# Two feed-forward up-projections of a four-block attention kernel: from a plain fp32 product to three rounded products over 128 rows

## The chip, the cores and the metric

One core of a Trainium2 chip. The metric is the device time of one execution in microseconds (us); the time before is the median of three runs. Engines: TensorE (PE in the rows; PEld is its weight load), VectorE (DVE), ScalarE (ACT), GpSimd (POOL) and SyncE (SP), on whose queue all DMAs of this kernel are issued.

## The reference

Four attention blocks run one after another on four batches of 256 rows of 160 values, with a context of 512 rows of 96 values (`B, SQ, D = 4, 256, 160`, `SK, C = 512, 96`). Blocks L1 and L3 are transformer blocks and end in a gated feed-forward half:

```
h1 = _ln(x, n1_g, n1_b)
x = _attn(h1, h1, q1, k1, v1, o1_w, o1_b, heads) + x
h2 = _ln(x, n2_g, n2_b)
x = _attn(h2, context, q2, k2, v2, o2_w, o2_b, heads) + x
h3 = _ln(x, n3_g, n3_b)
proj = h3 @ ff_w1 + ff_b1
a, g = jnp.split(proj, 2, axis=-1)
ff = a * jax.nn.gelu(g, approximate=False) @ ff_w2 + ff_b2
return ff + x
```

`ff_w1` is 160x1280 and `ff_w2` 640x160. Blocks L0 and L2 are attention with a residual; L2 adds a small second attention over four extra rows. All is fp32.

## The kernel before, in words

The work is 24 instances: six phases (`PHASES`) by four batches. Phase 0 is L0's attention, 1 and 2 the self and cross attention of L1, 3 the block L2 (with the small attention, unit 4), 4 and 5 those of L3. In an instance the heads go by fours (a "quad"). For a quad the keys are brought into a ring of four slots by four DMAs (`kdma`, ring L901); TensorE makes the scores once for the row maximum (`max`, L972, reduced on VectorE at L1428), transposes the negated maximum into the queries (`mtr`, L986, added at L1452), makes the scores again transposed (`st`, L952), ScalarE takes the exponential (`probs`, L1259), and TensorE multiplies by the values (`pv`, L1010) into `pv_ps`, read out by ScalarE (`oT`, L1268). L952 and L972 use tiles of 64 rows, L1010 column tiles, everything else the full array.

Scores are made from rounded operands (`FR`, fp32r), with a high and a low part stacked in the rows. Other products are plain fp32: `two_part` (L928, L929) multiplies an operand of 160 rows as two halves of 80. The up-projection is one of these: `ff_g` (the gate) and `ff_a` (the other half), ten column blocks of 128 in all for each feed, each `two_part` over 256 columns. One fp32 matmul is one row in the order but leaves two records in the trace.

A feed (`feed` in `behind`) is: `ln` (statistics, VectorE and GpSimd), `x_bias` (GpSimd, L1591), `norm` (VectorE, L1472), `h_tr` (transposes L1076, L1077; copy with the norm's scale and shift on ScalarE, L1320), three `ff_g` (ScalarE adds the bias, L1358), `gelu` (one ScalarE instruction over the buffer `gate`, 128x1280, L1365), three `ff_a` (VectorE, L1515), and `ff_o` (L1174, added to x at L1503). There are eight: tag `ff1` for four batches behind phase 2, `ff3` behind phase 5. The last one, `LAST_FEED`, has nothing beside it; there the gate and the other half alternate.

The order of every engine is written by a planner. `plan` gives each step a due time and puts the side steps into `stages`, lists whose steps go one after another; `simulate` walks a model of the engines, takes what can start first by `needs` (`data_needs`) and `cost`, and emits one list `order`. Each engine then runs its part of `order` strictly in that sequence. A step without TensorE work is taken as soon as its `needs` allow. `takes_buffer` locks a shared buffer: `gate` is one, and at the start it also holds the context of batches 1 to 3. Seven PSUM banks are handed round; a TensorE step waits for `bank_taken` of its bank and for those of its inputs.

The weights of a block come in three DMAs (`block_weights`: `wb`, `wd`, `wbc`), for L1 at the start, for L3 after the last `ff_o` of L1. `keep_clock` issues idle matmuls ahead of the last steps.

## Time and profile before

| | |
|---|---|
| runs before, us | 920.84, 926.18, 924.26; median 924.26 |
| profiled execution, us | 923.25 |
| its span, us | 921.3 |
| mean granted TensorE clock | 0.998 of full |
| busy share PE, PEld, DVE, ACT, POOL | 96%, 64%, 73%, 71%, 6% |
| instructions in the profile | 21210 |

The span runs from the first to the last instruction of the profiled execution; its own time is 1.95 us longer. Busy shares are unions of instruction times. TensorE's instructions are pipelined and overlap, so the step between two of them is read from their starts, not from their durations. The granted clock is the share of full speed that TensorE was given: 1.00 is 2.4 GHz, 0.50 is 1.2 GHz.

### The profile page before, as it was taken

The numbers are of one execution on the slowest core, as the hardware profiler recorded it, in microseconds if no ns is written. First come the engines' busy times: TensorE is split into PE (matmuls) and PEld (weight loads), VectorE is DVE, ScalarE is ACT, GpSimd is POOL, SyncE is SP. The second block draws the span as 40 slices with busy tenths as digits, with TensorE's granted clock in tenths as the row PEclk, the third lists the DMA queues.
The fourth block names the chain that finished last, engine by engine and source line by source line (L and its number), as shares of the span: only waits on it lengthen the run. The fifth ranks groups of instructions, "written<-read, shape, count | busy, mean of one in ns | idle before, by whom it ended". The sixth has DMA issues, their size and how long they took to land.

```text
span 921.3 us, 21210 instructions
## 1 busy us (share of the span) xinstructions
PE 880.2 (96%) x7810; PEld 594.2 (64%) x7810; DVE 669.9 (73%) x1607; ACT 654.7 (71%) x1423; POOL 55.3 (6%) x92
## 2 busy tenths in 40 slices
PE   8999999999999999999999999999999999999987
PEld 6656565666666577676667776665676666766655
DVE  3978878878788876657566667776777898686822
ACT  7677786877777777667777576676777777776652
POOL 2000000000000000000000000000000000000100
PEclk9999999999999999999999999999999999999999
DMA  8111121111111201001000300001102111111100
GB/s 292 43 36 36 36 47 24 24 29 24 27 44 33 47 22 26 19 18 36 13 1 2 124 3 2 22 11 28 30 19 47 36 32 28 31 36 24 31 9 7
DMA packets 25964, 32.21 MB, mean 35 GB/s; under 512 B 9220, under 2 KB 17416, under 8 KB 25608
## 3 DMA queue, kind: packets, MB, share of 16 engines
q1 hardware_dynamic: 25864, 30.86, 13.1%
q8 instruction: 64, 1.05, 0.5%
q14 instruction: 36, 0.29, 0.1%
HBM read 9.21 MB, written 0.66 MB: 11 GB/s over the span
## 4 chain that ended last, share of the span: by engine, by line
PE 79%; DVE 8%; ACT 8%; issue 4%; ACTq 0%; DVEq 0%
PE pv_ps L1010 17%; PE bank_ps L952 12%; PE bank_ps L972 11%; PE bank_ps L928 8%; PE bank_ps L929 7%; DVE mx L1428 5%; PE bank_ps L1057 5%; PE bank_ps L986 4%; ACT probs L1259 3%; PE bank_ps L1037 3%; PE bank_ps L1130 3%; PE bank_ps L1118 2%; PE bank_ps L1174 2%; ACT oT L1268 1%; PE bank_ps L1076 1%
## 5 line engine op out<-in xcount | busy, mean ns | idle before, releaser
L1428 DVE TENSOR_REDUCE mx<-bank_ps 128x1 f32<-128x512 f32 (+3 forms) x720 | 452.1, 682 | 91.0 <-PE bank_ps L972 89.6
L1259 ACT ACTIVATE probs<-bank_ps 128x512 f32<-128x512 f32 x736 | 380.9, 601 | 116.7 <-PE bank_ps L952 115.2
L1010 PE MATMUL pv_ps<-probs,v 128*9 128x256 f32 (+2 forms) x2944 | 199.3, 376 | 5.4 <-ACT probs L1259 2.3
L952 PE MATMUL bank_ps<-qT,ring 64*128 64x256 f32 x1280 | 171.0, 303 | 2.5 <-DVE gate L1515 1.0
L972 PE MATMUL bank_ps<-ring,qT 64*128 64x512 f32 (+1 forms) x800 | 168.4, 393 | 2.4 <-ACT kdense L1310 1.1
L952 PEld LDWEIGHTS bank_ps<-qT,ring 64*128 64x128 f32 x1280 | 128.6, 185 | 62.7 <-issue 22.3
L972 PEld LDWEIGHTS bank_ps<-ring,qT 64*128 64x128 f32 x800 | 87.3, 184 | 43.2 <-issue 19.6
L1010 PEld LDWEIGHTS pv_ps<-probs,v 128*9 128x9 f32 (+2 forms) x2944 | 57.4, 90 | 76.4 <-issue 22.7
L1310 ACT ACTIVATE kdense<-bank_ps 128x512 fp32r<-128x512 f32 (+2 forms) x116 | 58.3, 556 | 22.2 <-PE bank_ps L1057 21.8
L1234 ACT ACTIVATE ks<-bank_ps 128x320 fp32r<-128x320 f32 x80 | 35.7, 447 | 42.5 <-PE bank_ps L929 22.1
L1452 DVE TENSOR_TENSOR qT<-bank_ps,qT 128x256 fp32r<-128x256 f32 (+1 forms) x108 | 47.0, 436 | 23.6 <-PE bank_ps L986 23.2
L1057 PE MATMUL bank_ps<-identr,ks 128*128 128x128 f32 (+1 forms) x416 | 60.8, 283 | 2.4 <-DVE mx L1428 1.2
L1057 PEld LDWEIGHTS bank_ps<-identr,ks 128*128 128x128 f32 (+1 forms) x416 | 52.1, 191 | 10.2 <-DVE mx L1428 3.1
L986 PEld LDWEIGHTS bank_ps<-identr,mn 128*128 128x128 f32 (+1 forms) x248 | 37.4, 189 | 27.7 <-issue 10.3
L986 PE MATMUL bank_ps<-identr,mn 128*128 128x128 f32 (+1 forms) x248 | 52.8, 300 | 1.4 <-DVE mn L1443 0.6
L1268 ACT ACTIVATE oT<-pv_ps 128x256 f32<-128x256 f32 x108 | 43.2, 400 | 10.8 <-PE pv_ps L1010 10.2
L1573 POOL TENSOR_SCALAR rstd<-mv 128x2 f32<-128x2 f32 x24 | 5.3, 220 | 683.8 <-DVE mv L1466 683.8
L928 PE MATMUL bank_ps<-hT_out,wb 128*128 128x256 f32 x140 | 44.1, 397 | 1.8 <-ACT hT_out L1320 1.0
L1130 PE MATMUL bank_ps<-ident,oT 128*128 128x128 f32 x216 | 31.9, 280 | 12.6 <-ACT oT L1268 12.6
L929 PE MATMUL bank_ps<-hT_out,wb 128*128 128x256 f32 x140 | 41.6, 379 | 0.0
L1352 ACT ACTIVATE qT<-bank_ps 128x512 fp32r<-128x512 f32 (+1 forms) x68 | 33.4, 560 | 7.1 <-PE bank_ps L1118 6.7
L1118 PE MATMUL bank_ps<-identr,qs 128*128 128x128 f32 (+1 forms) x248 | 37.2, 285 | 0.0
(178 smaller groups left out, 1037.1 us busy)
## 6 DMA issues: line engine op xcount, KB each, us to landing
ring<-kdense SPq DMA_DIRECT2D x240, 64.0 KB, 2.0
ring<-kdense SPq DMA_DIRECT2D x160, 32.0 KB, 1.9
wb<-in_w_blk SPq DMA_DIRECT2D x2, 2240.0 KB, 8.4
wd<-in_w_down SPq DMA_DIRECT2D x2, 400.0 KB, 8.5
x<-in_x SPq DMA_DIRECT2D x4, 160.0 KB, 4.5
bias<-in_bias SPq DMA_DIRECT2D x1, 640.0 KB
...
```

Of the source, the lines that this page charges most:

```text
L928: pe.matmul(out, lhs[:, 0, :], rhs[:, 0, :], start=True, stop=False)
L929: return pe.matmul(out, lhs[:, 1, :], rhs[:, 1, :], start=False, stop=True)
L952: mm = pe.matmul(bank[0:kr, i * a["nq"]:(i + 1) * a["nq"]], key_op(n, h)[:, c * P:c * P + kr], query_rows(u, b, h), start=True, stop=True)
L972: mm = pe.matmul(bank[0:rows, j * a["nk"]:(j + 1) * a["nk"]], query_rows(u, b, h)[:, tt * P:tt * P + rows], key_op(n, h)[:, 0:a["nk"]], st ...
L986: mm = pe.matmul(bank[:, k * a["nq"] + i * P:k * a["nq"] + i * P + rows], m, identr[0:rows, 0:rows], start=True, stop=True)
L1010: mm = pe.matmul(pv_ps[32 * j:32 * j + a["dh"] + 1, 0:a["nq"]], v, probs[0:kr, s % N_P, i * a["nq"]:(i + 1) * a["nq"]], start=(c == 0), st ...
L1057: mm = pe.matmul(bank[:, k * SQ + t * P:k * SQ + t * P + kr], ks[0:kr, t, g * of(u):(g + 1) * of(u), :].rearrange("p h s -> p (h s)"), ide ...
L1118: mm = pe.matmul(bank[:, k * nq + i * P:k * nq + i * P + rows], query_stack(u, b)[0:rows, t, g * of(u):(g + 1) * of(u), :].rearrange("p h ...
L1130: mm = pe.transpose(bank[0:rows, k * P:(k + 1) * P], src, ident[:, :])
L1259: nc.scalar.activation(probs[0:kr, s % N_P, 0:w], bank[0:kr, 0:w], ACT.Exp, scale=float(a["dh"]) ** -0.5).then_inc(free, 1)
L1310: nc.scalar.activation(dst, bank[:, 0:n * SQ].rearrange("p (g k) -> p g k", g=n)[:, :, 0:w], ACT.Copy).then_inc(free, 1)
L1428: nc.vector.tensor_reduce(mx[b][0:rows, t, heads[0]:heads[-1] + 1:heads[-1] - heads[0] or 1], bank[0:rows, 0:a["hpm"] * a["nk"]].rearrange ...
```

## The change

The up-projection's operands are split into a rounded high part and a low part. `up` (fp32r, three slots) holds: slot 0 the high part of the first 128 rows of the weights, slot 1 their low part, slot 2 the remaining 32 rows three times over (high, low, high). `hx` holds the normed rows likewise: slot 0 high, slot 2 low of the first 128 rows, slot 1 the last 32 rows, high twice and low. A column block is then four fp32r matmuls of 128 rows and 256 columns instead of two fp32 ones.

The weights arrive by `w_in`: twice per block 128x1280 values (640 KB) into `gate`; ScalarE rounds them (`w_high`), VectorE subtracts (`w_low`). `h_tr` of a feed becomes `f_tr`, with a `low` step; `norm` of a feed applies scale and shift on VectorE, from `ff_ln`. `v20` and `v8`, the values for 20 and 8 heads, share `v_all`; GpSimd sets the columns of ones again where the layout changes (`new_sums`, six times). `wb` is 960 instead of 2240 wide.

```diff
+def rounded_weights(k):
+    return [(kind, k, part) for part in range(2) for kind in ("w_in", "w_high", "w_low")]
...
-        first = [("ln", tag, b), ("x_bias", tag, b), ("norm", tag, b), ("h_tr", tag, b)]
+        first = [("ln", tag, b), ("x_bias", tag, b), ("norm", tag, b), ("f_tr", tag, b)]
...
+    stages[2].append(([("ctx_tr", b) for b in range(B)], [rounded_weights(0)]))
+    spread(span[0][1], span[3][1], rounded_weights(0))
...
+        if (ph, b) == (3, B - 1):
+            stages[2].append(([], [rounded_weights(1)]))
+            spread(span[k][1], span[k + 2][1], rounded_weights(1))
...
+        if kind == "f_tr":
+            return [("norm", *step[1:])] + ([("ff_o", "ff3", B - 2)] if step[1:] == LAST_FEED else [])
         if kind in ("ff_g", "ff_a"):
-            return [("h_tr", *step[1:3])]
+            return [("low", ("f_tr", *step[1:3])), ("w_low", 0 if step[1] == "ff1" else 1, 1)]
...
+                    elif step[0] == "w_in":
+                        _, k, part = step
+                        if part:
+                            sp.wait_ge(S["up_ready"], value["up_ready", ("w_low", k, part - 1)])
+                        elif k:
+                            taken(sp, ("o_proj", 3, B - 1))
+                        else:
+                            for b in range(1, B):
+                                taken(sp, ("ctx_tr", b))
+                        sp.dma_start(gate_cols, io["w_up"][k, part]).then_inc(s_up, 16)
...
-                            mm = two_part(bank[:, k * SQ:(k + 1) * SQ], wb[:, :, wts("w1", lo, lo + P)], hidden(tag, b)[:, :, :])
+                            terms = ((0, 0), (0, 2), (1, 0), (2, 1))
+                            for j, (w, h) in enumerate(terms):
+                                mm = pe.matmul(bank[:, k * SQ:(k + 1) * SQ], up[:, w, lo:lo + P], hx[:, h, :],
+                                               start=(j == 0), stop=(j == len(terms) - 1))
...
+                    elif kind == "f_tr":
+                        bank, free = filled(act, step)
+                        nc.scalar.activation(hx[:, 0:2, :].rearrange("p i q -> p (i q)"), bank[:, :], ACT.Copy).then_inc(S["f_high"], 1)
+                    elif kind == "w_high":
+                        _, k, part = step
+                        act.wait_ge(s_up, 16 * (2 * k + part + 1))
+                        nc.scalar.activation(up[:, 2 * part, :], gate_cols, ACT.Copy).then_inc(S["up_high"], 1)
...
+                    elif step[0] == "f_tr":
+                        dve.wait_ge(S["f_high"], value["f_high", step])
+                        nc.vector.tensor_tensor(hx[:, 2, :], bank[:, 0:SQ], hx[:, 0, :].bitcast(F32), ALU.subtract)
+                        ins = nc.vector.tensor_tensor(hx[64:P, 1, :], bank[64:P, SQ:2 * SQ], hx[64:P, 1, :].bitcast(F32), ALU.subtract)
...
+                    elif kind == "w_low":
+                        _, k, part = step
+                        dve.wait_ge(S["up_high"], value["up_high", ("w_high", k, part)])
+                        if part == 0:
+                            ins = nc.vector.tensor_tensor(up[:, 1, :], gate_cols, up[:, 0, :].bitcast(F32), ALU.subtract)
+                        else:
+                            ins = nc.vector.tensor_tensor(up[32:64, 2, :], gate_cols[32:64, :], up[32:64, 2, :].bitcast(F32), ALU.subtract)
+                        ins.then_inc(S["up_ready"], 1)
...
+                        if tag in ("ff1", "ff3"):
+                            dve.wait_ge(s_blk[0 if tag == "ff1" else 1], 64)
+                            n = natural(tag, b)
+                            for t in range(TQ):
+                                ins = nc.vector.scalar_tensor_tensor(out=n[:, t, 0:D], in0=x[b][:, t, :], scalar=m[:, t, 0:1],
+                                                                     in1=ff_ln[:, 0, :], op0=ALU.subtract, op1=ALU.mult)
+                            link(ins)
+                            for t in range(TQ):
+                                ins = nc.vector.scalar_tensor_tensor(out=n[:, t, 0:D], in0=n[:, t, 0:D], scalar=r[:, t:t + 1],
+                                                                     in1=ff_ln[:, 1, :], op0=ALU.mult, op1=ALU.add)
+                            link(ins)
...
+                            nc.vector.tensor_copy(copies, again).then_inc(S["xn_ready"], 1)
```

`data_needs` has no entry for `w_in`, `w_high` and `w_low`: nothing tells the planner that `w_high` has to wait for its DMA, or `w_low` for `w_high`.

How that moves instructions is seen at three places. ScalarE near the start, in phase 0, where `ctxT` is the copy of the last context and `probs` the first exponentials. Before:

```order
L1272 ACTIVATE caT<-bank_ps 96x32 [waits bank_full1]
L1274 ACTIVATE ctxT<-bank_ps 96x512
L1324 ACTIVATE hT_in<-bank_ps 80x512 [waits bank_full6]
L1259 ACTIVATE probs<-bank_ps 128x512 [waits bank_full4]
L1259 ACTIVATE probs<-bank_ps 128x512 [waits bank_full3]
```

and now:

```order
L1334 ACTIVATE caT<-bank_ps 96x32 [waits bank_full0]
L1336 ACTIVATE ctxT<-bank_ps 96x512
L1393 ACTIVATE up<-gate 128x1280 [waits feed_forward_weights_in] x2
L1386 ACTIVATE hT_in<-bank_ps 80x512 [waits bank_full5]
L1321 ACTIVATE probs<-bank_ps 128x512 [waits bank_full3]
L1321 ACTIVATE probs<-bank_ps 128x512 [waits bank_full0]
```

Both roundings stand directly behind the copy that frees the buffer. In the same place VectorE has both subtractions in a row, and SP (the second fence) both DMAs, the second waiting for the first subtraction:

```order
L1499 TENSOR_REDUCE mx<-bank_ps 128x1 [waits bank_full3]
L1530 TENSOR_TENSOR up<-gate,up 128x1280 [waits up_high]
L1532 TENSOR_TENSOR up<-gate,up 32x1280 [waits up_high]
L1462 TENSOR_TENSOR ks<-bank_ps,ks 128x20x8 [waits k_high,bank_full1]
L1499 TENSOR_REDUCE mx<-bank_ps 128x1 [waits bank_full4]
```

```order
L953 DMA gate<-in_w_up 128x1280 [waits bank_taken0,bank_taken4,bank_taken2]
L953 DMA gate<-in_w_up 128x1280 [waits up_ready]
L937 DMA ring<-kdense 32x512 [waits bank_taken3]
```

The next key parts and maxima, and the ring DMAs from the third quad on, now stand behind them. VectorE in phase 4, where the output of L2's last batch is added to x, now:

```order
L1600 TENSOR_TENSOR x<-bank_ps,xb 128x320 [waits x_biased,bank_full6]
L1513 TENSOR_SCALAR mn<-mx 128x8 [waits bank_taken0]
L1514 SCALAR_TENSOR_TENSOR mn<-mx,mn 128x8 [waits dve_link]
L1530 TENSOR_TENSOR up<-gate,up 128x1280 [waits up_high]
L1532 TENSOR_TENSOR up<-gate,up 32x1280 [waits up_high]
L1542 BN_STATS stats<-x 128x6 [waits bank_taken6]
```

The same pair again, for block L3, three instructions behind the addition that releases the first DMA. TensorE in the first feed, before:

```order
L928 MATMUL bank_ps<-hT_out,wb 128x256 [waits bank_taken6,bank_taken3]
L929 MATMUL bank_ps<-hT_out,wb 128x256
L928 MATMUL bank_ps<-hT_out,wb 128x256
L929 MATMUL bank_ps<-hT_out,wb 128x256
```

and now, for the same two column blocks:

```order
L1225 MATMUL bank_ps<-hx,up 128x256 [waits up_ready,bank_taken5,bank_taken6]
L1225 MATMUL bank_ps<-hx,up 128x256 x7
```

Four fp32 matmuls became eight rounded ones. Counted over the whole order, TensorE changes between 64-row tiles, column tiles and the full array 747 times before and 729 times now.

## Rows read from the trace of the kernel before

**Rows 1.** The page: span, busy time and share of each engine, the chain.

```profile
span 921.3 us, 21210 instructions
PE 880.2 (96%) x7810; PEld 594.2 (64%) x7810; DVE 669.9 (73%) x1607; ACT 654.7 (71%) x1423; POOL 55.3 (6%) x92
...
PE 79%; DVE 8%; ACT 8%; issue 4%; ACTq 0%; DVEq 0%
PE pv_ps L1010 17%; PE bank_ps L952 12%; PE bank_ps L972 11%; PE bank_ps L928 8%; PE bank_ps L929 7%; DVE mx L1428 5%; PE bank_ps L1057 5%; PE bank_ps L986 4%; ACT probs L1259 3%; PE bank_ps L1037 3%; PE bank_ps L1130 3%; PE bank_ps L1118 2%; PE bank_ps L1174 2%; ACT oT L1268 1%; PE bank_ps L1076 1%
```

**Rows 2.** Stretches: start:end, us, busy us of each engine, clock, DMA, GB/s.

```profile
60.00:120.00 60.00, 58.69 (x566) 36.58 (x565) 50.59 (x116) 45.45 (x102) 1.81 (x3) 0.99 0.16 37
340.00:520.00 180.00, 173.87 (x1467) 121.57 (x1466) 115.45 (x269) 125.89 (x255) 7.89 (x12) 1.00 0.07 17
780.00:885.00 105.00, 102.55 (x884) 71.61 (x882) 76.39 (x166) 73.10 (x138) 6.10 (x9) 1.00 0.12 27
```

**Rows 3.** TensorE in a feed, in order of time: start us, us, line, count.

```profile
351.01 0.59 PE L929 MATMUL bank_ps<-hT_out,wb 128*128 128x256 f32 x2
351.44 0.59 PE L928 MATMUL bank_ps<-hT_out,wb 128*128 128x256 f32 x2
```

**Rows 4.** The chain: rounded matmuls in a row, start us, us on the chain.

```profile
672.61 0.98 PE bank_ps L952 x10
680.77 1.18 PE bank_ps L1057 x10
```

**Rows 5.** Groups by form, TensorE and VectorE: busy us, mean ns of one.

```profile
L928 PE MATMUL bank_ps<-hT_out,wb 128*128 128x256 f32 x140 | 44.1, 397 | 1.8 <-ACT hT_out L1320 1.0 <-DVE gate L1515 0.8
L1395 DVE TENSOR_TENSOR ks<-bank_ps,ks 128x160 fp32r<-128x160 f32 x76 | 23.0, 315 | 15.3 <-ACT v L1282 13.4 <-ACT v L1289 2.0
L1395 DVE TENSOR_TENSOR ks<-x,ks 128x320 fp32r<-128x320 f32 x4 | 1.9, 486 | 1.1 <-ACT v L1298 1.0
L1452 DVE TENSOR_TENSOR qT<-bank_ps,qT 128x256 fp32r<-128x256 f32 x100 | 41.5, 415 | 19.2 <-PE bank_ps L986 18.7
```

**Rows 6.** Groups by form, ScalarE.

```profile
L1365 ACT ACTIVATE gate<-gate 128x1280 f32<-128x1280 f32 x7 | 8.9, 1270 | 0.1
L1327 ACT ACTIVATE hT_out<-bank_ps 80x512 f32<-80x512 f32 x23 | 13.7, 597 | 3.8 <-PE bank_ps L1142 3.8
```

**Rows 7.** DMA issues: count, KB each, median us from issue to landing.

```profile
ring<-kdense SPq DMA_DIRECT2D x240, 64.0 KB, 2.0
wb<-in_w_blk SPq DMA_DIRECT2D x2, 2240.0 KB, 8.4
```

**Rows 8.** Stretches: the granted clock in phase 0, and block weights under way.

```profile
59.00:60.00 1.00, 1.00 (x3) 0.34 (x1) 0.43 (x1) 0.57 (x2) 0.00 (x0) 0.50 0.00 0
525.00:527.00 2.00, 2.00 (x18) 1.26 (x21) 1.36 (x6) 1.71 (x7) 0.00 (x0) 1.00 1.00 430
```

**Rows 9.** In order of time, where the first ring slot and the last context arrive.

```profile
24.15 1.74 PE L972 MATMUL bank_ps<-ring,qT 64*128 64x512 f32 x8 [1.07 <-ACT kdense L1310]
32.47 3.29 DVE L1428 TENSOR_REDUCE mx<-bank_ps 128x1 f32<-128x512 f32 x5
35.05 0.19 ACT L1272 ACTIVATE caT<-bank_ps 96x32 f32<-96x32 f32 x1 [0.37 <-PE bank_ps L1024]
35.14 0.58 ACT L1274 ACTIVATE ctxT<-bank_ps 96x512 f32<-96x512 f32 x1
```

**Rows 10.** In order of time, the addition of L2's last batch in phase 4.

```profile
627.47 0.49 DVE L1503 TENSOR_TENSOR x<-bank_ps,xb 128x320 f32<-128x320 f32 x1 [0.25 <-PE bank_ps L929]
```

**Rows 11.** In order of time, the last feed.

```profile
902.59 1.16 DVE L1472 TENSOR_SCALAR nat_in<-x,mv,rstd 128x160 f32<-128x160 f32 x2 [1.14 <-POOL rstd L1575]
904.82 1.01 ACT L1320 ACTIVATE hT_in<-bank_ps,lncols 80x256 f32<-80x256 f32 x2 [6.23 <-PE bank_ps L1077]
905.98 0.67 PE L928 MATMUL bank_ps<-hT_in,wb 128*128 128x256 f32 x2 [1.20 <-ACT hT_in L1320]
914.25 0.59 PE L929 MATMUL bank_ps<-hT_in,wb 128*128 128x256 f32 x2
```

108 lines of the change are left out of this document (76 added, 32 removed).

## The prediction

> **What bounds the kernel now.** I read the page first: TensorE is busy 96% of the span and holds 79% of the chain that ended last, VectorE and ScalarE 8% each [rows 1]. Then the stretches. Where feeds run, TensorE is busy 173.9 of 180 us and 102.6 of 105, VectorE 115.5 and 76.4, ScalarE 125.9 and 73.1. In phase 0, without a feed, VectorE reaches 50.6 of 60 while TensorE still shows 58.7 [rows 2]. So the feeds are the stretches in which TensorE is most alone at the limit, and the other two are idle for about a third of them. The two lines of `two_part` hold 8% and 7% of the chain [rows 1]. Against that stand the orders of the change, which put DMA-dependent steps in front of everything on three queues.
>
> About 0.5% (4.6 us) is what a measurement of this kernel can tell from no change.
>
> **1. The matmuls removed.** A feed has 10 column blocks of two fp32 matmuls, each with two records (140 records of L928 in seven feeds [rows 5]). Two records follow the last two at 0.43 us [rows 3], 0.216 us each; 40 records are 8.64 us a feed. The new block is four rounded matmuls of 256 columns with 128 weight columns. No such shape is in the trace. Near it are L952, 256 columns over 64 rows, ten in 0.98 us, and L1057, full 128x128 weights but 128 columns, ten in 1.18 [rows 4]: 0.10 and 0.12 us. I take 0.11, between the two since each shares one side of the shape: 40 cost 4.4 us, 4.24 saved. The far bound is 0.216, if a rounded matmul over all 128 rows went like one fp32 record; then nothing is saved.
>
> Seven feeds lie beside attention: 29.7 us. How much reaches the end? If 4.24 us leave each, four feeds take 17 us from the 180 us of phase 2, and VectorE's share there goes from 64 to 75%, below phase 0's 84% [rows 2]. Waits for it and ScalarE already hold 16% of the chain [rows 1], and grow. I take 85%: **-25.2 us** (65 to 100%: 19.3 to 29.7).
>
> **2. The last feed** is all path [rows 11]. Matmuls from 905.98 to 914.84: -4.24. The copy by ScalarE is one of 512 columns, 0.60 [rows 6], for 1.01 [rows 11]: -0.41. The norm is 1.16 there now; four VectorE instructions over 160 columns at 0.32, a copy of 128 and two links make 1.7: +0.55. The low part is two instructions like L1452, 0.42 each [rows 5]: +0.9 with its handoff. Sum **-3.2**.
>
> **3. Added work beside others.** Seven feeds give VectorE 0.6 to 1.1 us more for the norm and 0.84 for the low part, 12 us in all; ScalarE loses 0.4 us each. VectorE is idle a third of these stretches [rows 2], so most is hidden; a fifth is charged, **+2**. If that cover goes, it is 12. GpSimd's six fills of ones stand where the values of three instances before have been read out, which the planner demands of the projection beside them anyway; GpSimd is 6% busy [rows 1]: 0. The shared value buffer adds no order of its own.
>
> **4. The split of the weights: the wait that is added.** The planner does not know what these six steps wait for, so they stand in a row: DMA, rounding, subtraction, and again. Behind the waiting rounding on ScalarE stand all exponentials and copies; behind the subtractions on VectorE all maxima; behind the second DMA on SP all ring loads. Price: 64 KB land after 2.0 us and 2240 KB after 8.4 [rows 7], so 640 KB in 2.0 + 576/2176 x 6.4 = 3.7. A ScalarE pass over 1280 columns is 1.27 [rows 6]. VectorE: 486 ns for 320 columns and 315 for 160, 1.07 a column [rows 5], so 1.51 for 1280. Twice 3.7 + 1.27 + 1.51 = 13.0, with six handoffs of some 0.1 us 13.5 us from the buffer's release to the end of the second subtraction, and VectorE does nothing else from its place in the order to there.
>
> DMA and bytes can also be priced by a page: the Trainium skill, "DMA: Bandwidth & Descriptors", holds a core's share of HBM to about 358 GB/s and the fixed part near 2 us. By it each load would be an estimated 3.9 us and the sum 0.4 us higher per place; the rows show 430 GB/s while block weights came [rows 8], so the measurement speaks against it.
>
> First place, at 35.7 us, behind the copy of the last context [rows 9]: VectorE's run of maxima ended at 35.76, so it stands from about 36 to 49.2. TensorE can fill the free banks with maxima and two score slots, some 1.5 us, then waits. VectorE is itself near its limit in phase 0 [rows 2], so nothing is caught up: **+12**. Second place, from 628.0, the end of the addition of L2's last batch [rows 10]: TensorE still has transposes and a value product, some 3 us, before it needs a copy that stands behind the second rounding; ScalarE then has six copies to make up. **+11**. TensorE, idle for over 8 us, comes back at a lower clock. In the trace it stood at 0.50 from 58 to 61 us, after a stretch of maxima on VectorE [rows 8]; 3.4 us of that cost at most 1.7, and while banks are still filling less: **+1** for both. Bounds for the two places: 6 (if ScalarE and VectorE had slack like their 27 to 29% average [rows 1] and won it back) to 30.
>
> **5. Start and order.** The first ring slot was used at 24.15 after 1.07 us of idle TensorE [rows 9], behind the block weights on the same DMA queue; 1280 KB less now stand before it: **-1** (0 to -3). 18 of 747 changes of tile shape go. TensorE's idle time, 41 us, is 0.055 us a change if all of it is theirs [rows 1]; as much again may lie inside the busy time: 0.1 each, **-2** (0 to -4). A new order of everything can go 3 us either way.
>
> Sum: -25.2 - 3.2 + 2 + 24 - 1 - 2 = -5.4 on the profiled execution's 923.25: 917.9. That execution lies 1.0 us below the median of the runs shown (924.26), within their spread of 5.3. I say **918**.
>
> **Rivals.**
> (a) *Removed TensorE time is not on the path.* VectorE and ScalarE take over where the feeds run: each attention instance there still needs its maxima and exponentials, and VectorE gets 1.9 us more a feed. It decides if less than about 60% of the 29.7 us arrives. For it: rounds of maxima and `ring` waits on the chain, VectorE 84% busy in phase 0 with the same attention shape. Against it: 64 and 73% in these stretches [rows 2]. With 40% (-12), and the rest of the sum: 923.25 - 12 - 3 + 4 + 24 - 3 = 933. Slower. 14%.
> (b) *The loads are hidden.* If the ScalarE queue is itself late at both places by 8 us or more, the DMAs have landed when it comes, and VectorE would have waited anyway. The queue's lead decides. At 35 us ScalarE had waited 0.37 us for its input [rows 9], so it had none; in phase 4 five exponentials stand ahead of the rounding, 3 us of work. With 24 going to 4: 898. 13%.
> (c) *The clock.* Each stall leaves TensorE at half clock, and its restart, full of waits for copies, keeps it there for two or three such stretches of 3.4 us, a loss of up to 1.7 us each [rows 8]: +4 more, 922. The Trainium skill, "TensorE: Matmul & The Clock Gate", section "HAM oscillation", says that a wait for a DMA makes the next work start cold. The trace shows only one such stretch after a short stop, so recovery was quick there. No measurable change. 16%.
> (d) *The change does not do what it says*: rounded matmuls over 128 rows at 0.216 us. Then only costs are left, 923.25 + 2 + 24 - 2 = 947. Nothing in rows 4 looks like it. 3%.
>
> **How the numbers follow.** My forecast holds 54%: 910 to 925 by its own bounds, of which 43 parts lie below 919.6 and 11 above. With (b) faster is 56%; the 11 parts and (c) make 27% same; (a) and (d) 17% slower. The range must leave out no more than 2 in 10: from 906, which cuts off most of (b), to 929, which cuts off most of (a) and (d).
>
> **What would show it.** In the profile after: 320 records at the new matmul line, some 0.11 us apart; span shares of `two_part` down by 69 us of issue. Two gaps of 8 to 12 us in TensorE, near 37 and 610 to 630 us, with ScalarE waiting for the DMA of `gate` twice at each, and VectorE idle from before the first to after the second; granted clock 0.50 behind each. The phases 2 and 5 shorter by some 12 us each; from the last attention step to the store 3 us shorter. It is wrong if ScalarE shows no wait for that DMA, if the matmuls stand 0.2 us apart, or if TensorE's idle time in the feed stretches rises by what was removed.

## The result, and the profile after

Four runs of the changed kernel: 958.66, 958.93, 958.75 and 951.24 us, median 958.7; four of the kernel before beside them: median 922.61. The ratio is 1.0367, 95% interval 1.0305 to 1.0428. The kernel became 36 us slower; 918 (906 to 929) was predicted.

The profiled execution took 958.66 us. Its page, the lines that answer to [rows 1] and [rows 7], the slices of TensorE and of its clock, and the group of the new matmuls:

```profile
span 956.9 us, 21290 instructions
PE 877.8 (92%) x7810; PEld 595.4 (62%) x7810; DVE 687.1 (72%) x1653; ACT 657.6 (69%) x1419; POOL 56.3 (6%) x98
...
PE   8499999999999999899999999995999999999886
...
PEclk9789999999999999899999999967999999999899
...
PE 71%; ACT 11%; DVE 9%; issue 5%; DMA 2%; SPq 1%; ACTq 0%; POOL 0%; POOLq 0%; DVEq 0%
...
L1225 PE MATMUL bank_ps<-hx,up 128*128 128x256 f32 x320 | 43.9, 288 | 3.1 <-DVE hx L1481 1.7
...
gate<-in_w_up SPq DMA_DIRECT2D x4, 640.0 KB, 4.6
```

TensorE has two holes, in slices 2 and 28, and its clock falls around both and in places beside. The waits that were not there before, of ScalarE and of TensorE (in total, times, longest):

```profile
ACT up L1393 <- DMA gate<-in_w_up: 22.4, 4, 6.7
```

```profile
PE bank_ps L1019 <- DVE ks L1462: 14.5, 1, 14.5
PE bank_ps L999 <- ACT kdense L1372: 11.7, 1, 11.7
...
PE bank_ps L1019 <- DMA ring<-kdense: 3.9, 2, 3.0
PE bank_ps L1176 <- DVE gate L1612: 3.7, 2, 2.0
```

The first of them in order of time: two rounds of load, rounding, subtraction in a row, and TensorE idle from 35.0 to 49.5.

```profile
38.29 1.27 ACT L1393 ACTIVATE up<-gate 128x1280 fp32r<-128x1280 f32 x1 [3.90 <-DMA gate<-in_w_up]
39.59 1.49 DVE L1530 TENSOR_TENSOR up<-gate,up 128x1280 fp32r<-128x1280 f32 x1 [7.92 <-ACT up L1393]
...
46.27 1.27 ACT L1393 ACTIVATE up<-gate 128x1280 fp32r<-128x1280 f32 x1 [6.71 <-DMA gate<-in_w_up]
...
47.57 1.48 DVE L1532 TENSOR_TENSOR up<-gate,up 32x1280 fp32r<-32x1280 f32 x1 [6.49 <-ACT up L1393]
...
49.47 0.80 PE L1019 MATMUL bank_ps<-ring,qT 64*128 64x512 f32 x2 [14.52 <-DVE ks L1462]
```

**Where the time went, by stages.** Windows cut at the last read-out of a stage (start to the end of phase 1; phase 2 with feeds ff1; phases 3 and 4; phase 5 with feeds ff3; the tail). Columns: start:end, us, then busy us of TensorE and the others. Before, then after:

```profile
0.00:285.20 285.20, 271.58 (x2464) 176.44 (x2466) 223.27 (x530) 212.77 (x476) 19.29 (x34) 0.99 0.21 55
285.20:522.10 236.90, 229.93 (x1985) 158.62 (x1983) 165.20 (x390) 169.85 (x355) 12.28 (x19) 1.00 0.09 20
522.10:718.80 196.70, 188.76 (x1755) 129.52 (x1756) 144.33 (x379) 141.30 (x335) 12.34 (x21) 1.00 0.12 33
718.80:893.60 174.80, 169.78 (x1515) 114.54 (x1515) 130.54 (x291) 125.41 (x251) 9.63 (x15) 1.00 0.12 29
893.60:921.30 27.70, 20.16 (x96) 15.09 (x96) 6.58 (x20) 5.43 (x10) 1.75 (x3) 1.00 0.02 6
```

```profile
0.00:302.90 302.90, 275.10 (x2464) 179.52 (x2466) 226.64 (x530) 216.10 (x477) 19.21 (x34) 0.97 0.20 52
302.90:532.60 229.70, 216.96 (x1951) 152.25 (x1951) 166.84 (x400) 165.20 (x344) 11.98 (x21) 0.97 0.09 20
532.60:754.80 222.20, 202.06 (x1780) 139.53 (x1782) 153.16 (x396) 145.51 (x339) 13.79 (x25) 0.93 0.12 32
754.80:931.70 176.90, 167.13 (x1524) 111.68 (x1524) 132.01 (x305) 125.83 (x252) 9.61 (x15) 0.97 0.12 28
931.70:956.90 25.20, 16.53 (x96) 12.39 (x96) 8.45 (x25) 5.01 (x9) 1.75 (x3) 1.00 0.02 7
```

The two stages with a load are 17.7 and 25.5 us longer, the feeds gained 7.2 in phase 2 and lost 2.1 in phase 5, the tail gained 2.5.

**The same in three terms**, which all runs below are read by. *Idle*: span minus TensorE's busy time, both from the page. *Clock*: half of the time in which the granted clock is 0.50 and TensorE works. *Work*: what is left, TensorE's work at full clock. After, the clock is at 0.50 in nine stretches of 3.4 to 20.5 us, 78.5 us in all (half of that is the 4.1% that the mean clock of 0.959 lacks); 23 us of them are idle, so the term is 28.

| profiled execution, us | span | idle | clock | work |
|---|---|---|---|---|
| before | 921.3 | 41.1 | 1.7 | 878.5 |
| after | 956.9 | 79.1 | 27.7 | 850.1 |
| difference | +35.6 | +38.0 | +26.0 | -28.4 |

TensorE was relieved of 28 us, where the prediction had 33.9 (eight feeds of 4.24). It got 38 us of waiting and 26 us of half clock. The longest stretch, from 36.6 to 57.1, is mostly idle and costs 3.8 us of the 27.7, the one behind the second hole 2.1; the dearest is the 17.1 us from 630.5 to 647.6, ahead of the second hole, with 8.5.

How little the clock follows from what TensorE does at the moment: from 630.5 to 655.7, ahead of the second hole, TensorE is busy all the time and the clock is at half for 17 us of it (columns as above, the clock is the number after POOL).

```profile
49.50:57.10 7.60, 7.60 (x36) 5.42 (x40) 5.28 (x11) 3.39 (x6) 0.00 (x0) 0.50 0.01 3
...
630.50:655.70 25.20, 25.17 (x134) 17.15 (x134) 11.72 (x28) 10.63 (x23) 0.00 (x0) 0.66 0.09 21
```

### The profile page after: what moved, and what is told of

Read it like the earlier page. It is cut to its first block, busy times and chain, and to the rows that moved or that the text cites. A ratio compares the mean times of both kernels' runs of the same rounds, so it can differ in the third digit from the quotient of the medians.

```text
span 956.9 us, 21290 instructions
## 1 busy us (share of the span) xinstructions
PE 877.8 (92%) x7810; PEld 595.4 (62%) x7810; DVE 687.1 (72%) x1653; ACT 657.6 (69%) x1419; POOL 56.3 (6%) x98
## 4 chain that ended last, share of the span: by engine, by line
PE 71%; ACT 11%; DVE 9%; issue 5%; DMA 2%; SPq 1%; ACTq 0%; POOL 0%; POOLq 0%; DVEq 0%
PE pv_ps L1059 16%; PE bank_ps L999 11%; PE bank_ps L1019 11%; DVE mx L1499 5%; PE bank_ps L975 4%; PE bank_ps L1106 4%; ACT probs L1321 4%; PE bank_ps L976 4%; PE bank_ps L1033 3%; PE bank_ps L1188 3%; PE bank_ps L1086 3%; PE bank_ps L1236 3%; PE bank_ps L1176 2%; DMA gate<-in_w_up 2%; PE bank_ps L1225 2%
## 5 line engine op out<-in xcount | busy, mean ns | idle before, releaser
L1059 PE MATMUL pv_ps<-probs,v_all 128*9 128x256 f32 (+2 forms) x2944 | 203.9, 382 | 4.9 <-ACT oT L1330 2.5
L1019 PE MATMUL bank_ps<-ring,qT 64*128 64x512 f32 (+1 forms) x800 | 167.5, 402 | 22.5 <-DVE ks L1462 14.5
L999 PE MATMUL bank_ps<-qT,ring 64*128 64x256 f32 x1280 | 173.4, 307 | 15.3 <-ACT kdense L1372 11.7
L999 PEld LDWEIGHTS bank_ps<-qT,ring 64*128 64x128 f32 x1280 | 131.5, 189 | 72.7 <-issue 16.3
L1019 PEld LDWEIGHTS bank_ps<-ring,qT 64*128 64x128 f32 x800 | 87.7, 190 | 67.7 <-issue 29.6
L1059 PEld LDWEIGHTS pv_ps<-probs,v_all 128*9 128x9 f32 (+2 forms) x2944 | 58.1, 92 | 75.6 <-issue 21.4
L1106 PE MATMUL bank_ps<-identr,ks 128*128 128x128 f32 (+1 forms) x416 | 63.7, 287 | 1.3 <-DVE ks L1462 1.0
L1106 PEld LDWEIGHTS bank_ps<-identr,ks 128*128 128x128 f32 (+1 forms) x416 | 54.2, 195 | 11.6 <-DVE mx L1499 2.9
L1523 DVE TENSOR_TENSOR qT<-bank_ps,qT 128x256 fp32r<-128x256 f32 (+1 forms) x108 | 47.1, 436 | 19.1 <-PE bank_ps L1033 18.4
L1330 ACT ACTIVATE oT<-pv_ps 128x256 f32<-128x256 f32 x108 | 43.4, 402 | 17.9 <-PE pv_ps L1059 17.7
L1225 PE MATMUL bank_ps<-hx,up 128*128 128x256 f32 x320 | 43.9, 288 | 3.1 <-DVE hx L1481 1.7
L1225 PEld LDWEIGHTS bank_ps<-hx,up 128*128 128x128 f32 x320 | 39.6, 189 | 7.4 <-DVE hx L1481 1.9
```

The lines of the kernel that those rows point to most:

```text
L999: mm = pe.matmul(bank[0:kr, i * a["nq"]:(i + 1) * a["nq"]], key_op(n, h)[:, c * P:c * P + kr], query_rows(u, b, h), start=True, stop=True)
L1019: mm = pe.matmul(bank[0:rows, j * a["nk"]:(j + 1) * a["nk"]], query_rows(u, b, h)[:, tt * P:tt * P + rows], key_op(n, h)[:, 0:a["nk"]], st ...
L1059: mm = pe.matmul(pv_ps[32 * j:32 * j + a["dh"] + 1, 0:a["nq"]], v, probs[0:kr, s % N_P, i * a["nq"]:(i + 1) * a["nq"]], start=(c == 0), st ...
L1106: mm = pe.matmul(bank[:, k * SQ + t * P:k * SQ + t * P + kr], ks[0:kr, t, g * of(u):(g + 1) * of(u), :].rearrange("p h s -> p (h s)"), ide ...
L1225: mm = pe.matmul(bank[:, k * SQ:(k + 1) * SQ], up[:, w, lo:lo + P], hx[:, h, :], start=(j == 0), stop=(j == len(terms) - 1))
L1523: nc.vector.tensor_tensor(q, bank[:, 0:(g1 - g0) * nq], q.bitcast(F32), ALU.add).then_inc(done, 1)
```

## Experiments

Theory at this point: the two stalls, with the half clock behind them, are the loss, and the feeds give their gain back. Rivals: the added VectorE work, the new order, the removed time not being on the path. Of every run the median is given, and its ratio to runs of the kernel before that were taken beside it, with a 95% interval. Those runs had medians of 925.6 to 927.5 us in the experiments, so two experiments of different sessions are better compared by their ratios than by their microseconds. Where idle, clock and work are named, they are those of one profiled execution each.

### The stalls

**e1: no loads and splits**, the order of the steps unchanged.

```diff
                     elif step[0] == "w_in":
+                        continue
...
+                nc.gpsimd.memset(up[:, :, :].bitcast(F32), 0.0625).then_inc(s_up, 1)
```

> The changed kernel with its order of every engine kept, but without the six steps that load and split the up-projection's weights (both DMAs, both roundings, both subtractions, for both blocks); up is filled with a constant once, so the feeds compute with other weights. Theory A (the two stalls and the half clock behind them cost 37 us, the gap between instances that the trace of the changed kernel shows at both places): 958.7 - 35 = about 922 us, two long idle stretches of TensorE gone, the half-clock stretches of 20.5, 17.1 and 13.7 us gone with them. Rival B (the new order itself is slow, the stalls only coincide): above 940 us.

919.86 us, ratio 0.9959 (0.9913 to 1.0004). The six steps cost 39 us, not 24. Of the 40.7 us between the two profiles 25.0 are idle and 18.0 clock (work is 2.3 up in e1). Of the clock, 5.9 stand directly behind the two stalls and 8.5 in the stretch at 630.5. e1 itself is not a gain all through: its phase 2 is 9.1 us shorter than before, but the stages without a feed are longer, the start to the end of phase 1 by 1.5 and phases 3 and 4 by 3.9 us, with more TensorE work in both though none was added there:

```profile
0.00:286.70 286.70, 273.58 (x2464) 178.64 (x2466) 223.96 (x528) 214.18 (x475) 22.56 (x35) 0.99 0.20 51
...
514.50:715.10 200.60, 191.63 (x1780) 132.63 (x1782) 150.37 (x395) 143.11 (x338) 13.84 (x25) 1.00 0.11 28
```

**e10: only the second load.** The `continue` only for `k == 0`.

> The changed kernel with the first load and split of the weights left out (the first feeds' weights are a constant, filled by GpSimd) and the second one kept where it is. Left out of the computation: the first feeds' weights. If the two stalls add: the profiled runs of the changed kernel and of the first experiment differ by 40.7 us, of which the stage with the second stall has 21.7, so 939 to 943 us. If the second stall costs only its idle time of 11.7 us and the rest came from the first: 930 to 934.

934.34, ratio 1.0106 (1.0075 to 1.0137). The second place costs 14 us, so the first 24. The stalls don't simply add: of the 25 us between the two profiles, 17.0 lie in the stage of the first load, but 7.6 in the stage of the second, which both kernels do in the same order; the half clock there is 33.0 us in one and 17.1 in the other. It is the stretch at 630.5 that e10 does not have, and e8 (next) does not have it either. So it is not shown to come from a stall; of the four runs of the changed kernel one took 951.24 us at a mean clock of 0.968 where the others had 0.959.

**e8: the first stall filled** with TensorE work.

```diff
+                        if (n, i) == (1, 5):
+                            for _ in range(16):
+                                pe.matmul(pv_ps[:, :], ident[:, :], wc[:, 0:512], start=True, stop=True)
```

> The changed kernel, with 16 full-precision products of 512 columns (about 0.86 us each, 13.8 us in all) put into TensorE's first idle stretch of 14.5 us, into an output that nothing has used by then: the stretch is as long as before but TensorE is busy in it, so its clock should stay at the full level. Nothing of the computation is left out. Theory A (the first stall costs more than its idle time because of the half clock that starts in it, 36.6 to 57.1): the half-clock stretch of 20.5 us goes, the stage is 4 to 8 us shorter, and the time is 951 to 955 where the changed kernel has 958.7. Theory B (the clock in the stage does not matter since ScalarE and VectorE, late by the same stall, set its pace): no half clock there and the time within 2 us of 958.7.

953.57, ratio 1.0299 (1.0267 to 1.0331). The number is that of theory A, but the run doesn't show it: the clock was full in the stall, and had been at half before it, so TensorE came to the place 5.7 us later and the stage was not shorter (205.0 us to the end of phase 0; after: 202.3). What it gained lies later: the stage of the second stall is 7 us shorter (214.9 against 222.2), without the 17 us of half clock that the changed kernel has ahead of that stall, from 630.5.

```profile
25.00:38.70 13.70, 13.70 (x46) 10.53 (x45) 6.18 (x13) 6.45 (x16) 0.00 (x0) 0.50 0.00 0
40.70:54.70 14.00, 14.00 (x36) 6.07 (x34) 3.44 (x4) 3.02 (x3) 0.00 (x0) 1.00 0.46 132
```

What the half clock behind the first stall costs by itself stays open.

**e4: the planner told what the steps wait for**; nothing of the computation is left out.

```diff
+        if kind == "w_in":
+            _, k, part = step
+            return [("w_low", k, 0)] if part else [("o_proj", 3, B - 1)] if k else [("ctx_tr", b) for b in range(1, B)]
+        if kind == "w_high":
+            return [("w_in", *step[1:])]
+        if kind == "w_low":
+            return [("w_high", *step[1:])]
```

> The changed kernel, with the planner told what the six steps wait for (DMA before rounding, rounding before subtraction, first subtraction before the second DMA); all computed as in the change. The order puts exponentials and maxima between them. Theory A (stalls were the loss): like e1 plus the six passes beside other work, 920 to 928 us, no idle stretch of TensorE over 4 us. Rival B (the loads hurt by the DMA queue, delaying ring loads behind 640 KB each): above 935 us with TensorE waiting for the ring.

924.27, ratio 1.0004 (0.9973 to 1.0035). Past the start no idle of TensorE over 3.0 us is left: with the three missing data needs put in, the loss against the kernel before is gone. (e4 has yet another order of the steps; how much that alone brings or costs is not separated.) But this is only even with the kernel before, with 25 us less work for TensorE (853.7): idle 53.6, clock 14.6.

### Where the feeds' gain goes

**e2: the kernel before with half the products** of the up-projection.

```diff
-                            mm = two_part(bank[:, k * SQ:(k + 1) * SQ], wb[:, :, wts("w1", lo, lo + P)], hidden(tag, b)[:, :, :])
+                            mm = pe.matmul(bank[:, k * SQ:(k + 1) * SQ], wb[:, 0, wts("w1", lo, lo + P)], hidden(tag, b)[:, 0, :],
+                                           start=True, stop=True)
```

> The kernel before with one fp32 matmul per column block of the up-projection instead of two (the second half of the rows is left out of the product); order, waits and all else as before. It takes 8 x 10 x 0.432 = 34.6 us of TensorE time out of the feeds. Theory A (TensorE time in the feeds lies on the path, 85% beside attention, all of it in the last feed): 922.6 - 30 = 893 us. Rival B (the time comes back as waits for VectorE and ScalarE and as half clock): 910 to 920 us, with new idle stretches of TensorE over 1 us and new stretches at 0.50 in phases 2 and 5.

912.01, ratio 0.9855 (0.98 to 0.991): of 34.6 us removed, 13.6 arrive, 39%. In the profile: work -29.6, idle +12.8, clock +6.8. So the kernel before, with nothing of the change in it, gives back over half of the TensorE time taken out of its feeds. TensorE's waits for VectorE's products were 1.8 us in all before; now they are 8.6:

```profile
PE bank_ps L1164 <- DVE gate L1516: 5.7, 3, 2.4
PE bank_ps L952 <- DVE gate L1516: 2.9, 2, 1.9
```

**e3: e1 with the four terms made twice.**

```diff
+                            terms = 2 * terms
```

> As e1_nostall, but with eight instead of four rounded matmuls per column block (the four terms twice), so that a feed's up-projection takes the 8.8 us of TensorE that it took before the change. Theory A (on the path): e1 + 7 x 4.4 x 0.85 + 4.4 = e1 + 30 us. Rival B (the feeds are not bound by TensorE, and the half-clock stretches there come from its having less to do): e1 + 0 to 10 us, and the stretches at 0.50 near the feeds disappear.

947.2, ratio 1.027 (1.0185 to 1.0354). Against e1, 35 us of TensorE work cost 27; taking 34.6 from the kernel before brought 13.6. TensorE's waits for VectorE's products, 8.7 us in e1, are gone. The run is some 22 us slower than the kernel before. Of the 18.4 us between the two profiles 9.0 are TensorE work (eight matmuls at 0.12 us take longer than four records at 0.216), 4.4 idle and 5.1 clock. So some 10 us of idle and clock come with the order and the added VectorE work alone, with no product saved.

**e5: e1 with less VectorE work ahead of the products.**

```diff
-                                ins = nc.vector.scalar_tensor_tensor(out=n[:, t, 0:D], in0=x[b][:, t, :], scalar=m[:, t, 0:1],
-                                                                     in1=ff_ln[:, 0, :], op0=ALU.subtract, op1=ALU.mult)
...
+                                ins = nc.vector.tensor_scalar(n[:, t, 0:D], x[b][:, t, :], m[:, t, 0:1], r[:, t:t + 1],
+                                                              ALU.subtract, ALU.mult)
...
-                        nc.vector.tensor_tensor(hx[:, 2, :], bank[:, 0:SQ], hx[:, 0, :].bitcast(F32), ALU.subtract)
```

> As the first experiment (the changed kernel in its own order, without the loads and splits of the weights, which are filled with a constant), and VectorE's added work in front of the products is taken out too: the two scale-and-add passes of four operations (390 ns each) become one pass of two as in the kernel before, and one of the two subtractions that form the low parts of the activations (427 ns) is left out, its operand filled with zeros. Some 1.6 us of VectorE less in each of the 8 feeds, 13 us in all; TensorE's work is the same. Left out of the computation: the learned scale and bias of the normalization, a low part, and the weights. Theory A (step 3 of the prediction was mis-sized: the added VectorE work is in the path of the feeds, where TensorE now waits for VectorE's buffers): 8 to 12 us less than the first experiment's 919.9, near 910, about what the kernel before with half the products took (912). Theory B (the added work is hidden; what TensorE saves comes back as the clock's half-rate stretches and waits for the planned order): within 3 us of 919.9.

913.98, ratio 0.9877 (0.9852 to 0.9902): 5.9 us less than e1 by the medians, 7.6 by the ratios, 3.9 between the profiles, so between the two theories. By the rows what went is 4 x 390 - 2 x 400 + 427 = 1.2 us a feed, 9.5 us in all (not the 13 of the expectation). By an estimate from these numbers 40 to 80% of it reached the end.

**The chain behind Gelu.** The waits in e1's feed show one thing that holds TensorE. First the kernel before, in the first feed, in order of time: ScalarE loads Gelu's table and applies it while TensorE makes the five blocks of the other half, 4.3 us; VectorE's products begin before TensorE is done.

```profile
354.53 1.28 ACT L1365 ACT_TABLE_LOAD   x1
354.55 0.65 PE L928 MATMUL bank_ps<-hT_out,wb 128*128 128x256 f32 x2
...
355.82 1.27 ACT L1365 ACTIVATE gate<-gate 128x1280 f32<-128x1280 f32 x1
...
357.21 0.87 DVE L1515 SCALAR_TENSOR_TENSOR gate<-bank_ps,cols,gate 128x256 f32<-128x256 f32 x2 [2.03 <-ACT gate L1365]
...
358.67 0.59 PE L929 MATMUL bank_ps<-hT_out,wb 128*128 128x256 f32 x2
```

Then e1 at the same place (its five blocks, four matmuls each, began at 356.04):

```profile
357.23 1.28 ACT L1433 ACT_TABLE_LOAD   x1
358.52 1.27 ACT L1433 ACTIVATE gate<-gate 128x1280 f32<-128x1280 f32 x1
359.90 2.05 DVE L1612 SCALAR_TENSOR_TENSOR gate<-bank_ps,cols,gate 128x256 f32<-128x256 f32 x5 [4.82 <-ACT gate L1433]
360.83 1.34 PE L1086 MATMUL bank_ps<-wbc,ctxT 128*128 128x320 f32 x4 [2.17 <-DVE gate L1612]
```

TensorE is through at 358.7, holds its banks until VectorE has emptied them, and stands 2.2 us at the next projection. The saved products had been the cover of table load and Gelu. To test it:

**e13 and e14: Gelu replaced by a copy**, in e1 and in the kernel before.

```diff
-                        nc.scalar.activation(gate[:, :, :], gate[:, :, :], ACT.Gelu).then_inc(S["gate_ready"], 1)
+                        nc.scalar.activation(gate[:, :, :], gate[:, :, :], ACT.Copy).then_inc(S["gate_ready"], 1)
```

> The first experiment (no loads and splits of weights, 919.9 us) with the Gelu over a feed's 1280 columns on ScalarE replaced by a copy of the same columns, in the seven feeds that have that step: its two function-table loads (1.28 us each, 14 in all) go, so VectorE's products and behind them TensorE's banks are ready 1.3 us earlier. Left out of the computation: Gelu in seven of eight feeds, and the weights. Theory A (what TensorE saves in the feeds comes back because its second half of the blocks now ends before ScalarE's table load and Gelu do, which had been hidden behind 4.3 us of products): the waits before products' banks shrink from some 2 us to under 1, the half-clock stretches behind them go too, and the time is 903 to 910, with a gain over its base that is 5 to 10 us larger than that of the run beside it on the kernel before. Theory B (the waits are set elsewhere): both kernels gain the same, 3 to 6 us, 914 to 917.

> The kernel before with the same replacement of Gelu by a copy in seven of eight feeds; that is what is left out of the computation. The control for the run beside it. Theory A: the Gelu is hidden behind TensorE's products here, so the gain is small, 0 to 4 us: 921 to 926. Theory B: as much as in the run beside it, 919 to 922.

e13: 906.18, ratio 0.9762 (0.9727 to 0.9797), 13.7 us less than e1 by the medians and by the profiles, 18 by the ratios. e14: 925.36, ratio 0.9964 (0.9936 to 0.9992), 3 us less than before. The same 18 us of ScalarE are worth at least four times as much in the changed kernel; theory A holds. e13 against e1: idle -8.5, clock -4.6, work the same. The waits for VectorE's products fall from 8.7 us to 1.7. Of the clock, 2.9 come from half-clock stretches that are shorter behind two waits for the ring (see below), which e13 still has; that this is Gelu's doing is not shown. TensorE's waits for VectorE's `gate`, in e1:

```profile
PE bank_ps L1176 <- DVE gate L1612: 3.7, 2, 2.0
...
PE bank_ps L1086 <- DVE gate L1612: 2.2, 1, 2.2
```

and VectorE's wait for Gelu in e1, then in e13:

```profile
DVE gate L1612 <- ACT gate L1433: 18.8, 7, 4.8
```

```profile
DVE gate L1612 <- ACT gate L1433: 7.8, 3, 3.4
```

**Two waits that come with the order.** e1's longest two idles are not of this chain. At both, eight ring loads stand on SP's queue right behind another DMA: once a small load that had waited for VectorE's `qs`, once the store of a batch that had waited for its last addition. TensorE's next scores need the ring:

```profile
377.02 0.26 SPq L902 DMA_DIRECT2D ca_n<-in_ctx  x1
377.38 4.94 SPq L937 DMA_DIRECT2D ring<-kdense  x8
...
381.32 0.79 PE L1019 MATMUL bank_ps<-ring,qT 64*128 64x512 f32 x2 [2.95 <-DMA ring<-kdense]
```

```profile
844.21 0.40 SPq L961 DMA_DIRECT2D out_rows<-x  x1
844.71 4.94 SPq L937 DMA_DIRECT2D ring<-kdense  x8
...
848.62 0.79 PE L1019 MATMUL bank_ps<-ring,qT 64*128 64x512 f32 x2 [2.41 <-issue]
```

The profile names no releaser for the second wait; that it is the ring load is read from the order of events. Both have 6.8 us of half clock behind them. Together they are 5.4 us of idle and 6.3 of clock, against 8.7 and 1.7 for the waits behind VectorE's products. In the changed kernel they are there too (2.95 and 2.41 us), and in e3 as well (2.97 and 3.86), whose products are as long as before or longer: they do not come from the shorter products. In the kernel before and in e2 the same DMAs go in the same row, and TensorE has no wait for the ring behind them.

### The clock

**e9: unused products in front of five waits of e4**; nothing of the computation is left out.

```diff
+                cover = {("max", 52, 0): 3, ("max", 113, 0): 3, ("kv_proj", 2, 3, 2): 2, ("q_tr", 3, 1, 0): 2, ("q_tr", 6, 3, 0): 2}
...
+                    pe.wait_ge(bank_taken[b], k)
+                    for _ in range(cover[step]):
+                        pe.matmul(bank_ps[b][:, :], ident[:, :], wc[:, 0:512], start=True, stop=True)
```

> The fourth experiment (924.3 us; nothing of the computation left out) with full-precision products of 512 columns, whose result is never used, put in front of the five steps at which TensorE waits 1.7 to 3.0 us in its trace and after which its clock is at half: three each before the scores of quads 52 and 113, two each before one projection of keys and values and two transposes of queries, into a bank that is already free. The dozen products are 10 us of TensorE work that fit into waits of 11.4 us. The half-clock stretches behind those five waits are 6.8, 3.4, 6.8 and 3.4 us (a fifth wait has its stretch in common with one). Theory A (the short waits let the clock fall, and the half clock is a part of what the feeds give back): these stretches go, worth half their length, about 10 us, and the time is 912 to 917. Theory B (the clock's half stretches are not brought by these waits, or come back elsewhere): within 3 us of 924.3; if the added products come late into the waits, up to 5 us more.

920.23, ratio 0.9946 (0.992 to 0.9973); 4 us less than e4 by the medians and 5 by the ratios, half of what theory A gave. In the profile idle -8.6, work +10.7, clock -7.8. The stretches behind the covered waits near 378, 785 and 851 are gone; the one of a cover that stood a step too early stayed, with its wait. Two of the five are the ring waits above. Two stretches of 3.4 us are there that e4 had not, at 469.8 and 637.1, and one that no cover stood before, at 908.8, is gone.

**e15: that cover set right, and one more.**

```diff
-("q_tr", 3, 1, 0): 2
+("q_tr", 3, 1, 1): 2, ("ff_g", "ff3", 3, 0): 2
```

> The ninth experiment (920.2 us; nothing of the computation left out) with the unused products put at two more waits: in front of the second group of query transposes of one instance, where they had stood one step too early (wait of 1.8 us, 3.4 us of half clock behind it), and before the first products of the last feed (1.7 us). Theory A (half clock follows such waits): one or two stretches less, 1.7 to 3.4 us: 917 to 919. Theory B: 920 to 922.

917.52, ratio 0.9886 (0.9856 to 0.9915): the fastest kernel that computes everything, some 1% below the kernel before and 41 us below the change as it was made. The covered stretch is gone; of the three that are left, one, at 509.1, is new.

### The order

**e6 and e7: the planner's costs set to what was measured**, in e4 and in the kernel before.

In e7 this is the whole edit; in e6 the other costs of its expectation are set too.

```diff
-        return n * f32(2 * SQ), (act if kind == "ff_g" else dve)(*n * [SQ])
+        return n * f32(2 * SQ), [("act", n * 490)] if kind == "ff_g" else [("dve", n * 477)]
```

> The fourth experiment (the loads and splits of the weights given their data needs in the planner, so that other work is planned beside them) with the planner's costs for the new steps set to what the trace of the changed kernel measured: ScalarE's bias step of a block 490 ns where it had 273, VectorE's product 477 where it had 329, the normalization 1800 where it had 1126, the ScalarE copy behind the transposes 616 where it had 487, the low parts 345 each, the load 4600. Nothing of the computation is left out. Theory A (TensorE's savings are lost because the plan underrates ScalarE and VectorE in the feeds, so waits follow that it did not plan): 5 to 10 us less than the fourth experiment's 924.3, so 914 to 919, below the kernel before. Theory B (the waits are those of the feed's own chain, whatever the plan): 920 to 928.

> The kernel before, with only the planner's costs of the feed's blocks corrected (490 and 477 ns where it had 273 and 329): the control for the run beside it. Nothing of the computation is left out. If better costs alone were worth something whatever the change does: 915 to 920. If they matter only where TensorE is short of work: within 3 us of the kernel before (920 to 927).

e6: 953.43, ratio 1.0321 (1.026 to 1.0383). e7: 948.67, its four runs from 936.51 to 957.73, so no interval. Both theories of both runs fall: costs nearer to the measured ones made both kernels much slower. The profile of e7, 936.51 us: work -1.7, idle +7.2, clock +7.8.

**e11 and e12: the kernel before, planned with a cost of the changed one.**

```diff
-        return n * f32(2 * SQ), (act if kind == "ff_g" else dve)(*n * [SQ])
+        return n * 4 * 107, (act if kind == "ff_g" else dve)(*n * [SQ])
```

> The kernel before, all its work unchanged, but the planner told that the products of a feed's block take as long as in the changed kernel (428 ns a column block in place of 855), which gives another order of the steps from step 1205 of 2995 on. Theory A (a new order costs time by itself, 10 to 25 us as in the run with corrected costs, whatever the work): 932 to 950. Theory B (an order made for the right costs is what counts, and this one is only a little off): 922 to 930.

> The kernel before, all its work unchanged, but the planner told the longer normalization of the changed kernel (1.1 us in place of 0.54), which changes the order from step 1133 on. A second draw of the same question as the run beside it: Theory A, 932 to 950; Theory B, 922 to 928.

e11: 930.25, ratio 1.006 (1.0025 to 1.0095). e12: 934.84, ratio 1.0102 (1.0052 to 1.0152). With e7 that is three new orders of unchanged work, and each is slower, by 5 to 23 us; e11 is within a quarter of a microsecond of its theory B, e12 in the range of theory A.

**e16: a data need that makes the second half of the products wait for Gelu.**

```diff
+            after_gelu = [("gelu", *step[1:3])] if kind == "ff_a" and step[1:3] != LAST_FEED else []
+            return [("low", ("f_tr", *step[1:3])), ("w_low", 0 if step[1] == "ff1" else 1, 1)] + after_gelu
```

> The fourth experiment (924.3 us; nothing of the computation left out) with one more data need in the planner: the second half of a feed's products waits for Gelu, so that TensorE takes other work in the meantime and these products don't hold three banks that VectorE can't empty yet. Another order of the steps follows. Theory A (the waits behind Gelu are what eats TensorE's saving, and a plan can fill them): 908 to 918. Theory C (every new order costs 5 to 23 us beside the one of the kernel before, as the three runs of it with other costs did): 926 to 945.

940.46, ratio 1.0135 (1.0097 to 1.0173). Both theories have a part. Phase 2 in e4 and in e16, then phases 3 and 4 of e16, and a piece of them:

```profile
286.50:513.90 227.40, 214.62 (x1951) 150.52 (x1952) 166.46 (x400) 165.09 (x345) 11.98 (x21) 0.98 0.09 20
```

```profile
286.80:508.80 222.00, 213.54 (x1925) 147.06 (x1925) 163.84 (x391) 163.67 (x342) 11.93 (x21) 0.98 0.09 20
508.80:738.00 229.20, 214.67 (x1806) 146.74 (x1807) 157.35 (x405) 145.69 (x342) 13.83 (x25) 0.91 0.11 31
598.40:615.50 17.10, 15.52 (x106) 10.15 (x110) 9.40 (x18) 6.17 (x16) 0.00 (x0) 0.50 0.01 2
```

The feeds gained 5.4 us in phase 2 and 4.6 in phase 5; the stage between, which has no feed, is 229.2 us long where e4 has 204.3, with 41 us of half clock. One stretch of 17 us began there with an idle of only 0.64 us just before it.

**e17: e16 with unused products before eight of its waits.**

> The sixteenth experiment (940.5 us; nothing of the computation left out), whose feeds did gain (its stages with the feeds ff1 and ff3 took 222.0 and 172.5 us where the fourth has 227.4 and 177.1) but whose stage between them had 41 us of half clock and was 25 us longer. Unused full-precision products are put in front of eight of its waits, one or two each, 12 us of TensorE work where it idles some 14 us. Theory A (the loss of that stage is half clock behind short waits, and the waits can be covered): 10 to 15 us of the 31 us that the clock costs go, 922 to 930. Theory B (the half clock in that stage, of which 17 us began without a wait of 0.8 us or more, comes from the small products of the stage and not from the waits): 936 to 942.

930.28, ratio 1.006 (1.0029 to 1.009), 10 us less than e16: in the profile clock -23.3, idle -8.6, work +17.4. Half clock can be bought off with unused products: 17.4 us of added work took away 23.3 us of clock and 8.6 of idle.

**e18: e15 with ScalarE's Gelu ahead of the work that stood between it and the last bias step.**

```diff
+    for step in [s for s in order if s[0] == "gelu"]:
+        order.remove(step)
+        order.insert(order.index(("ff_g", *step[1:], 2)) + 1, step)
```

> The fifteenth experiment (917.5 us; nothing of the computation left out) with one thing moved: ScalarE does a feed's Gelu right behind the feed's last bias step, not after the one to five evictions and exponentials that the plan had put between them (0.4 to 2.5 us). Theory A (the chain of Gelu and VectorE's products is what TensorE waits for): up to 1.5 us a feed in the four feeds where it waits, less what the moved-back evictions cost: 912 to 916. Theory B (the unused products already cover those waits, and the evictions behind Gelu are now late for TensorE): 917 to 922.

928.89, ratio 1.0022 (1.0002 to 1.0042), 11 us more than e15 and worse than either theory: idle +7.7, clock +8.4. The work moved behind Gelu was needed sooner than Gelu: TensorE now waits for ScalarE's exponentials 3.8 us at 506.8 and 3.4 us at 838.7, where e15 has neither wait.

## Why the prediction was wrong, step by step

The forecast was 41 us too low. Steps 1, 2, 3 and 5 add up to -29.4 us; e1, which has just these, is 5.1 us below the kernel before in its profile, and its interval of 0.9913 to 1.0004 hardly tells it from no change. That is 24 us of the miss. Step 4, +24, cost 39: 15 to 17 us more.

**Step 1, the matmuls removed: the share wrong, the price a little low.** The new matmuls follow each other at 0.12 us (median 0.119), not 0.11, so 31 us were to be had and not 33.9. In e1 work is only 26.1 less, because it went up by some 5 us in the stages without a feed; idle is 13.0 more and clock 8.0. But 85% was to reach the end, and in e2, without any other part of the change, it is 39%. The step that failed is the reading of shares: VectorE at 75% is below phase 0's 84%, so it has room. The room was there on average; the limit was a chain inside a feed (bias steps, table load, Gelu, VectorE's products, the banks) of which the products were the cover. TensorE's waits for VectorE's products are 1.8 us before, 8.6 in e2, 8.7 in e1, none in e3 and 1.7 in e13. The trace of before had shown the chain: VectorE already waited 23.2 us for Gelu in its seven feeds. It is a question of a place, and was answered by a mean.

**Step 2, the last feed: near.** The tail is 27.7 us before and 25.2 after, -2.5 for -3.2.

**Step 3, added VectorE work, +2: too small.** It was priced as hidden at four fifths, and each of the norm's four passes takes 0.39 us where 0.32 was taken. e5 took 9.5 us of it out and gained 4 to 8, so of the some 15 us added (1.0 for the norm and 0.85 for the low part in each of eight feeds) an estimated 6 to 12 reach the end.

**Step 4, the split of the weights: the stall right, what it costs not.** The order, the two places and ScalarE's two waits at each were as described. From the buffer's release to the end of the second subtraction it took 14.7 and 15.3 us, 13.5 predicted; a load took 4.6 us, not 3.7, and the page of the Trainium skill named in the prediction came nearer (3.9) without reaching it. TensorE stood 14.5 and 11.7 us for +12 and +11, and e1 against after has 25.0 us of idle: so far the step holds. The term that failed is "+1 for both" for the clock: it is 18.0 us between these two profiles. It was made from one stretch of 3.4 us in [rows 8]; after, the clock fell to half from 36.6 to 57.1 and from 657.8 to 671.5, and ahead of the second stall from 630.5 to 647.6. Directly behind the stalls stand 5.9 us of it and in the stretch at 630.5, whose cause stays open, 8.5.

**Step 5, start and order, -3: the start right, the order not.** The first ring slot came 1.0 us earlier (23.13 against 24.15), as predicted. The 18 fewer changes of tile shape were to bring 2 us of TensorE time; nothing shows them, and in e1 the stages without a feed have more work. "A new order can go 3 us either way" is far too narrow: three orders of the same work cost 5, 9 and 23 us (e11, e12, e7), and in this one the two ring waits alone are 11.7 us of e1's profile.

**The rivals.** (b) and (d) are out: ScalarE waited 22.4 us for the four loads, and the matmuls stand at 0.12 us. The number of (d), 947, was nearest to 958.7, but by luck. (c), the clock, was a real mechanism and was priced at 4 us more; 18.0 went with the six steps, of 26 in all. The Trainium skill has both forms of it: "TensorE: Matmul & The Clock Gate", sections "HAM oscillation" (a wait for a DMA makes the next work start cold) and "A second HAM failure mode: psum-queue depth-cycling" (short idles of TensorE between groups as banks go round). By the first, the trace agrees: 14.5 us idle behind a DMA, 20.5 at half clock, 7.6 of them with work. By the second, the trace agrees in part: waits of 2.0 to 3.0 us for VectorE's banks and ring slots (at 374.8, 396.1, 477.0 and 887.5) each had half clock behind them, but e1's wait of 2.17 us at 358.7 had none. The condition of (a), under 60% of the time arriving, was met, but VectorE and ScalarE did not take over by being full: VectorE is busy 73% of the span before and 72% after. It was latency, at single places.

That the range ended at 929 is from taking (a) and (c) as alternatives. They came together, with the stalls under both; yet (a) with the 4 us of (c) is 937, so the sizes were too small as well. Of the signs that the prediction named, "the phases 2 and 5 shorter by some 12 us each" failed most plainly: one is 7.2 us shorter, the other 2.1 longer.
